# Edge weights from a second sort by run length, and the cell plan interleaved with the first convolution, in a graph network on one core

## The reference

```
h    = einsum('ni,rio->nro', x, weight)            # 8 transformed copies of each node
msg  = h[src, etype]
seg  = dst * R + etype
cnt  = segment_sum(ones, seg, N * R)               # edges per destination and type
norm = 1.0 / maximum(cnt[seg], 1.0)
agg  = segment_sum(msg * norm[:, None], dst, N)    # + x @ root + bias
# batch norm and relu after layers 0 and 1; x = layernorm(x + ...)
# then: h = x @ W_in + b_in; three times cur = segment_sum(cur[col] * w, row)
```

## Time and profile before

| | us |
|---|---|
| median of 3 runs | 5821.75 |
| lowest, highest | 5773.89, 5822.26 |
| profiled execution | 5815.68 |
| its span in the trace | 5813.9 |

### The profile page before, as it was taken

The page is one execution under the profiler, slowest core; times in us unless marked ns, Lnnn a source line. Parts: engine busy times, 40 slices in busy tenths (PEclk is TensorE's granted clock), DMA queues, the critical chain, the costliest instruction groups (busy, mean ns, idle before and its releaser), DMA issues.

```text
span 5813.9 us, 83767 instructions
## 1 busy us (share of the span) xinstructions
PE 4224.2 (73%) x16606; PEld 2206.6 (38%) x16607; DVE 3527.3 (61%) x10864; ACT 1456.7 (25%) x2714; POOL 2642.4 (45%) x2646
## 2 busy tenths in 40 slices
PE   7475576766766777677776786767677768989797
PEld 3122344444444333333333333333333333444343
DVE  8878644444445466666666556666666666364464
ACT  4465000000001333333333333333333340000000
POOL 0540466666665266666666436666666620000000
PEclk9678677777777998998899899998989889989898
DMA  6000111111111533333333353333334337969795
GB/s 215 8 11 6 30 45 45 45 45 45 45 45 41 200 120 118 118 119 119 118 119 118 123 196 116 119 119 119 119 117 120 117 109 248 301 225 301 234 300 170
DMA packets 416890, 716.88 MB, mean 123 GB/s; under 512 B 99201, under 2 KB 322742, under 8 KB 416330
## 3 DMA queue, kind: packets, MB, share of 16 engines
q1 hardware_dynamic: 332344, 545.52, 27.7%
q0 software_dynamic: 83984, 165.63, 11.4%
q10 hardware_dynamic: 130, 0.80, 0.0%
HBM read 431.69 MB, written 279.83 MB: 122 GB/s over the span
## 4 chain that ended last, share of the span: by engine, by line
PE 49%; issue 19%; DVE 14%; SPq 7%; another core or an unknown queue 5%; ACT 3%; DVEq 2%; DMA 1%; ACTq 0%
PE psum L961 15%; PE psum L1008 7%; PE psum L1009 7%; PE psum L948 6%; SPq L475 4%; PE psum L938 4%; SPq L476 3%; PE psum L909 3%; PE psum L842 2%; ACT bufE L655 2%; DVE area L1553 2%; PE psum L807 2%; DVE agg_and L1586 2%; DMA counts<-bufE 1%
## 5 line engine op out<-in xcount | busy, mean ns | idle before, releaser
L607 POOL DMA_INDIRECT area<-msg_table,visit_src x2490 | 2481.2, 996 | 1829.1 <-issue 581.4
L961 PE MATMUL psum<-area 128*128 128x256 f32 x4980 | 1713.8, 460 | 278.0 <-DVE agg_and L1586 247.0
L655 ACT CAST bufE<-psum 128x512 f16<-128x512 f32 x1507 | 883.3, 586 | 1761.3 <-PE psum L948 763.5
L961 PEld LDWEIGHTS psum<-area 128*128 128x128 f32 x4980 | 1046.5, 229 | 485.1 <-DVE agg_and L1586 279.4
L948 PE MATMUL psum<-bufE,carry 128*128 128x512 f16 x1506 | 643.6, 427 | 770.4 <-issue 461.7
L1586 DVE TENSOR_TENSOR agg_and<-agg_and,psum 128x256 f32 x1245 | 523.9, 421 | 770.6 <-PE psum L961 340.4
L1008 PE MATMUL psum<-area,edge_area 128*128 128x512 f16 (+1 forms) x1911 | 693.0, 370 | 81.2 <-DVE edge_area L1616 75.4
L948 PEld LDWEIGHTS psum<-bufE,carry 128*128 x1506 | 147.5, 98 | 1500.8 <-issue 1494.9
L1553 DVE SCALAR_TENSOR_TENSOR area<-iota,agg_and,psum 128x256 f32<-128x256 f32 x830 | 355.8, 478 | 558.6 <-remote 250.4
L1009 PE MATMUL psum<-area,edge_area 128*128 128x512 f16 (+1 forms) x1911 | 692.3, 370 | 0.0
L938 PE MATMUL psum<-bufE 128*128 128x512 f16 x1507 | 626.7, 416 | 0.7 <-issue 0.7
(11 more groups left out here) (318 smaller groups left out, 3077.1 us busy)
## 6 DMA issues: line engine op xcount, KB each, us to landing
area<-counts SPq DMA_DIRECT2D x252, 896.0 KB, 4.5
counts<-bufE SPq DMA_DIRECT2D x1507, 128.0 KB
msg_table<-area SPq DMA_DIRECT2D x147, 512.0 KB, 2.6
area<-msg_table,visit_src POOLq DMA_INDIRECT x2490
agg_and<-counts SPq DMA_DIRECT2D x162, 128.0 KB, 4.4
area<-counts SPq DMA_DIRECT2D x21, 224.0 KB, 3.4
bufE<-inv_sqrt SPq DMA_DIRECT2D x2, 1568.0 KB, 10.1
out<-cur SPq DMA_DIRECT2D x12, 256.0 KB
```

Source lines behind the costliest of these rows:

```text
L607: g.indirect_dma_start(out=msg[:, n % MV, :], out_offset=None, in_=msg_table, in_offset=bass.IndirectOffsetOnAxis(ap=visit_src[:, v:v + 1] ...
L655: a.copy(kept[:, m % KR, :], psum[:, 4 + m % 3, :]).then_inc(block_kept, 1)
L961: t.matmul(psum[:, banks[c % len(banks)], at:at + W2], msg[:, n % MV, :], visit_sel[:, n % SV, :], start=v % 2 == 0, stop=v % 2 == 1).then ...
```

## The change

1. `count_types`, its reciprocals, their way through DRAM, and in layer 0 the turning of types, their copies and the products with `inv_count` are gone.
2. In their place VectorE sorts the edges of each partition a second time, by destination, type and source (`group_edges`), and finds each run's length with one scan and ten shifted minima (`find_runs`). A run that crosses a partition's first or last destination is completed by counts of the eight types at both ends (`share_ends`), summed over partitions by four small products (`spread_ends`). The reciprocal is a third word of each edge.
3. Edges go to a new DRAM array `visit_rows` of three words, stored by ScalarE once the weights are known; GpSimd waits for that before the seven tile loads. `turn_tiles` turns three words instead of two, `keep_visits` copies `norm` out of PSUM.
4. `plan_cells` is cut into nine steps that run on VectorE after chunks 4, 14, ... 84 of layer 0, their TensorE products two chunks after each (`PLAN`, `plan_step`, `plan_product`).
5. Layer 0 uses four banks and adds three chunks late, as the other layers do, and selects with `norm`. The weights of layer 1 are made before `keep_visits`.
6. The ranking branch for unsorted edges is written anew, with two rounds; it is skipped with these edges. `load_tiles` no longer waits for the last addition of layer 0.

```diff
-MAIN = ((0, 1), (0, 1, 2, 3), (0, 1, 2, 3))
-SPREAD = (2, 3, 6)
+BANKS = (0, 1, 2, 3)
-LAG = (2, 3, 3)
+LAG = 3
+PLAN = tuple(range(4, 4 + 9 * 10, 10))
...
             pool.wait_ge(visits_planned, 1)
+            pool.wait_ge(rows_out, 16)
             for j in range(VB):
                 g.indirect_dma_start(out=runs[:, j, :, :].rearrange("p e w -> p (e w)"), out_offset=None,
-                                     in_=edge_rows.rearrange("(t e) w -> t (e w)", e=128),
+                                     in_=visit_rows.rearrange("(t e) w -> t (e w)", e=128),
...
             act.wait_ge(rows_ready, 1)
-            act.dma_start(edge_rows[0:E, :].rearrange("(p c) w -> p (c w)", p=EP), payload[:, :, :].rearrange("p c w -> p (c w)")).then_inc(rows_out, 16)
-            count_low()
-            keep_types()
+            act.dma_start(visit_rows[0:E, :].rearrange("(p c) w -> p (c w)", p=EP), edge_words[:, :, :].rearrange("p c w -> p (c w)")).then_inc(rows_out, 16)
...
+            def spread_ends():
+                pe.wait_ge(ends_ready, 1)
+                for j in range(2):
+                    last = t.matmul(psum[0:EP, 6, 128 * j:128 * j + EP], ones[0:EP, 0:EP], end_rows[:, j, :], start=True, stop=True)
+                last.then_inc(ends_spread, 1)
+                pe.wait_ge(shares_ready, 1)
+                for j in range(2):
+                    for h in range(2):
+                        last = t.matmul(psum[0:EP, 7, R * j:R * j + R], end_same[:, 2 * j + h, :], shares[:, 0, h, :], start=h == 0, stop=h == 1)
+                last.then_inc(shares_summed, 1)
...
                 for c in range(NQ):
+                    sums(c)
                     if k == 0:
-                        if c + 2 < NQ:
-                            turn_types(c + 2)
-                        if c + 1 < NQ:
-                            if (c + 1) % 2 == 0:
-                                pack = pack_of(c + 1)
-                            spread_weights(c + 1, pack)
-                    sums(c)
+                        plan_product(c)
...
+            def group_edges():
+                keys, spare = ungrouped.bitcast(I32), part(cur, 0, EC, dt=I32)
+                dve.wait_ge(x_turned, NXT)
+                link(v.tensor_scalar(keys[:, 0:EC], dst_i, GROUP_BITS + TYPE_BITS, KEY, ALU.logical_shift_left, ALU.bitwise_or))
+                link(v.tensor_scalar(spare, type_i, GROUP_BITS, None, ALU.logical_shift_left))
+                link(v.tensor_tensor(keys[:, 0:EC], keys[:, 0:EC], spare, ALU.bitwise_or))
+                link(v.tensor_tensor(keys[:, 0:EC], keys[:, 0:EC], src_i, ALU.bitwise_or))
+                link(v.memset(ungrouped[:, EC:SORT], NO_GROUP))
+                sort_keys(ungrouped, grouped)
+                keys = grouped.bitcast(I32)[:, 0:EC]
+                link(v.tensor_scalar(group_i, keys, GROUP_BITS, (1 << 16) - 1, ALU.logical_shift_right, ALU.bitwise_and))
+                link(v.tensor_copy(group, group_i))
...
+            def find_runs():
+                link(v.memset(same[:, 0:1], 0.0))
+                link(v.tensor_tensor(same[:, 1:EC], group[:, 1:EC], group[:, 0:EC - 1], ALU.is_equal))
+                link(v.tensor_tensor_scan(run_place, same, ones[0:EP, 0:1].to_broadcast([EP, EC]), 0.0, ALU.mult, ALU.add))
+                for buf in next_end:
+                    link(v.memset(buf[:, EC:1312], BIG))
+                frm, to = next_end
+                link(v.scalar_tensor_tensor(out=frm[:, 0:EC - 1], in0=same[:, 1:EC], scalar=BIG, in1=iota_visit[0:EP, 0:EC - 1], op0=ALU.mult, op1=ALU.add))
+                link(v.memset(frm[:, EC - 1:EC], float(EC - 1)))
+                for bit in range(LEVELS):
+                    link(v.tensor_tensor(to[:, 0:EC], frm[:, 0:EC], frm[:, 1 << bit:(1 << bit) + EC], ALU.min))
+                    frm, to = to, frm
+                link(v.tensor_tensor(run_place, run_place, iota_visit[0:EP, 0:EC], ALU.subtract))
+                link(v.tensor_tensor(run_place, run_place, frm[:, 0:EC], ALU.add))
+            def share_ends():
+                own, missing = shares[:, 0, :, :], shares[:, 1, :, :]
+                for j in range(2):
+                    for k in range(R):
+                        link(v.tensor_scalar(in_end[:, j, k, :], group, end_groups[:, j, k:k + 1], 0.0, ALU.is_equal, ALU.add, accum_out=own[:, j, k:k + 1]))
...
+            def find_norms():
...
+                for j in range(2):
+                    for k in range(R):
+                        link(v.scalar_tensor_tensor(out=run_place, in0=in_end[:, j, k, :], scalar=missing[:, j, k:k + 1], in1=run_place, op0=ALU.mult, op1=ALU.add))
+                v.reciprocal(edge_words[:, :, 2], run_place).then_inc(rows_ready, 1)
...
+            group_edges()
+            spread_ends()
+            find_runs()
+            share_ends()
+            decode_edges()
+            find_norms()
+            split_sources()
...
+            def plan_step(c):
+                if c == PLAN[0]:
+                    find_firsts()
+                elif c == PLAN[1]:
+                    find_cuts()
+                elif c == PLAN[2]:
+                    find_reach()
+                elif c == PLAN[3]:
+                    keep_dst_row()
...
+                elif c == PLAN[6]:
+                    find_tiles()
+                elif c == PLAN[7]:
+                    find_slots_of_blocks()
+                elif c == PLAN[8]:
+                    pack_carries()
...
-                        if k == 0:
-
-                            dve.wait_ge(weight_rows, q + 1)
-                            v.scalar_tensor_tensor(out=to, in0=iota[:, 0:W2], scalar=low, in1=psum[:, SPREAD[q % len(SPREAD)], at % 2 * W2:(at % 2 + 1) * W2],
-                                                   op0=ALU.is_equal, op1=ALU.mult, accum_out=norm[:, at:at + 1]).then_inc(visit_ready, 1)
-                        else:
-                            v.tensor_scalar(to, iota[:, 0:W2], low, norm[:, at:at + 1], ALU.is_equal, ALU.mult).then_inc(visit_ready, 1)
+                        v.tensor_scalar(to, iota[:, 0:W2], low, norm[:, at:at + 1], ALU.is_equal, ALU.mult).then_inc(visit_ready, 1)
...
+            make_weights(1)
             keep_visits()
```

495 lines of the change are left out of this document (222 added, 273 removed).

## The result

The changed kernel takes **5568.11 us** (median of 4 runs, 5565.44 to 5571.31), the kernel before 5803.24 (median of 4, 5773.89 to 5822.26) on the same chip: ratio **0.9596, 95% interval 0.9556 to 0.9637**. The prediction was 5424 with a range of 5355 to 5510. It is faster, as forecast, but by 235 us and not by 398 (the forecast started from a median of 5821.75).

What follows compares the result with a forecast made beforehand. No engine was near its limit; GpSimd lost time before the first gather and waiting for TensorE in layer 0. From 5815.7 us, 229.7 + 158.4 + 9.6 = 397.7 less gives 5418, plus 6 for the median: 5424, range 5355 to 5510.

Steps and rivals of the forecast that it cites:

- The preparation: Everything before layer 0's gathers: first gather at 400 us in place of 629.65, 229.7 us earlier.
- The scan: One scan of 800 elements on VectorE in finding runs: between 1.0 and 4.2 us, taken as 1.8.
- `rows_out`: GpSimd's added wait for stored edges before its tile loads: costs nothing, with 12 us to spare.
- The keys: GpSimd's key writes beside the sort: start 2.5 us earlier, slowed by 10 us (bounds nothing and 22), done at 373.5.
- Rival B: In the preparation, sort and key writes block each other: VectorE 82 us later, first gather 470, total 5494; chance 0.06.
- The last 5.7 us: End of the preparation: bases ready at 388 to 392, together with the tiles, then 9.2 us to the first gather at 400.
- Layer 0: First to last gather: GpSimd's pace of 1.284 us a gather stays, 1070 us in place of 1228.4, 158.4 us less.
- the bank rule: In layer 0, two banks keep TensorE from starting a chunk before the addition two chunks back; 247 us of waits, ended by four.
- The tail: From layer 0's last gather to its last addition: 6 us in place of 15.6, 9.6 less.
- A: Layer 0 keeps part of its pace through the chain of select, sum and addition: total 5454 to 5582; chance 0.17.
- D: The plan in layer 0 isn't hidden: 70 us of VectorE and 34 of TensorE on the path, total 5510; chance 0.05.
- C: Sorted rows make gather transfers slower in layers 0 to 2, so the kernel gets slower than before; chance 0.02.

Runs made afterwards that it cites:

- e7: Against the changed kernel, layer 0 sums into two banks and adds two groups behind, in place of four and three; layer 0 took 1196.6 us.
- e6: Against the changed kernel, TensorE in layer 0 waits for all four gathers and selections of a group before its first sum; layer 0 took 1196.7 us.
- f2: Against the changed kernel, VectorE makes 8 of the 256 columns of each selection in layer 0, for timing only; layer 0 took 1191.2 us.
- e2: Against the changed kernel, all plan steps and their products run ahead of the loop of layer 0; 5645.6 us, layer 0 1262.3 us.
- h1: The changed kernel itself, unaltered, run again on one chip with h2; 5568.41 us, ratio 0.9596 to the kernel before.
- h2: Against the changed kernel, 8 gather buffers in place of 16 and the degree count in layers 1 and 2 only; 5547.77 us, ratio 0.9565.
- f3: Against the changed kernel, TensorE in layer 0 sums only the last visit of each group of four, for timing only; layer 0 took 1188.9 us.

## Why the prediction was right and where it was wrong

**The preparation, right: 224.0 us earlier, 229.7 predicted.** Key writes by tile and GpSimd's timeline after, which answer to the earlier trace rows:

```profile
L547 POOL DMA_INDIRECT key_list<-edge_area x112: 1183/1191/1875, 188.3 to 377.7; - x112
```

```profile
379.17 0.98 POOL L603 DMA_INDIRECT bufE<-visit_rows,visit_tile  x1 [0.30 <-issue]
386.73 0.95 POOL L603 DMA_INDIRECT bufE<-visit_rows,visit_tile  x1 [0.30 <-issue]
405.69 0.95 POOL L577 DMA_INDIRECT area<-msg_table,visit_src  x1 [18.00 <-DVE agg_and L1547]
```

VectorE's timeline at the same place, and three groups of the preparation:

```profile
338.35 5.16 DVE L1335 RECIPROCAL bufD<-cur 125x800 f32<-125x800 f32 x1
386.15 1.66 DVE L1056 TENSOR_SCALAR area<-bases_sb,comp_sb 128x128 f32<-128x128 f32 x8 [40.58 <-DMA bases_sb<-in_L_gnn_bases]
387.84 7.51 DVE L1058 SCALAR_TENSOR_TENSOR area<-bases_sb,comp_sb,area 128x128 f32<-128x128 f32 x24
395.48 0.75 DVE L1533 MEMSET bufE<- 128x832 f32 x1
```

```profile
L1122 DVE TENSOR_TENSOR bufD<-bufD 125x512 f32<-125x512 f32 x55 | 38.5, 700 | 1.9
L1335 DVE RECIPROCAL bufD<-cur 125x800 f32<-125x800 f32 x1 | 5.2, 5155 | 0.0
L1290 DVE TENSOR_TENSOR_SCAN cur<-cur,ones 125x800 f32<-125x800 f32 x1 | 1.8, 1824 | 0.0
```

- The edges were ready at 343.51 us, where the reciprocal ends; predicted 346. The scan that the prediction bounded at 1.0 to 4.2 and took at 1.8 took 1.82, the reciprocal 5.16 (5.3 taken).
- `rows_out` cost nothing, as said: the first tile load follows the last key write by 0.30 us.
- The keys ended at 378.9, not 373.5. They started 4.6 us earlier (2.5 predicted), and 111 intervals took 189.4 us in place of 171.6: 18 us more, where 10 were taken, inside the bounds of 0 and 22. The sort steps themselves took 0.700 and 0.683 us, 0.693 and 0.685 before.
- Rival B (sort and keys block each other) did not come: not the step of VectorE is held up but the key write. Its mean was 1.43 us beside sort steps, 1.74 and 1.75 beside the 800-wide two-input steps L1334 and L1297, 1.19 beside the reciprocal. The Trainium skill, "SBUF — State Buffer", section "Who interferes with whom", names this pair. The trace agrees that the two contend, and not that whichever comes second is blocked for the whole instruction: sort steps beside a key write took 0.69 us, as without one, and the worst write, beside steps of 1.05 us, took 1.875 us against 1.19, 0.69 us more.
- The last 5.7 us: what ended last was the bases' path by way of SyncE, 395.4 in place of 388 to 392, because it hangs on the last key; from there to the first gather it was 10.3 us where 9.2 were taken.

**Layer 0, wrong: 32.0 us less, 158.4 predicted. This is the step that failed**: "TensorE no longer bounds it at either level, and four banks take away the wait of the earlier trace rows. GpSimd's pace is what stays ... 1.284 us". The measured 1196.4 us are 829 times the undisturbed interval of 1.252, 1038; 49 us by which gather instructions were longer than their median; and 110 of stops (predicted: 1065 with 17 of the second in it, and 5 for stops). The 49 are mostly the degree count: 1.62 us (mean of 45) for a gather beside its comparisons, 0.946 beside nothing; I had added 0.02 a gather from layer 1's mean. The 110 are the real error. In the kernel before GpSimd stood 1.1 to 2.2 us at 105 gathers, 86 of them exactly eighth ones, with two banks; I read the list of waits as the cause of these stops, and the bank rule as what would end them. They did end, and 48 irregular ones of 1.0 to 4.6 us took their place, 46 of them for the late signal of a sum that had long ended. e7 shows that the layer has the same length with the two banks kept. That signals can be late by the whole stock of buffers is in no term of the prediction.

**The tail, wrong sign:** 21.6 us, 15.0 before (the prediction counted 15.6, with the addition itself), 6 predicted. Last rows of layer 0:

```profile
1602.05 0.95 POOL L577 DMA_INDIRECT area<-msg_table,visit_src  x1 [0.31 <-issue]
1605.36 1.19 PE L905 MATMUL psum<-area 128*128 128x256 f32 x2 [0.74 <-DMA area<-msg_table,visit_src]
1611.08 0.42 DVE L1602 TENSOR_TENSOR agg_and<-agg_and,psum 128x256 f32 x1 [12.88 <-remote]
1622.38 0.42 DVE L1602 TENSOR_TENSOR agg_and<-agg_and,psum 128x256 f32 x1 [10.17 <-remote]
```

TensorE's last sum ended at 1606.55 by the records, "close behind the gathers" as predicted, but the addition could start only at 1622.38.

**The rivals.** A came true in its time (5454 to 5582) and in its place, and the "remote" waits named for it were the hint; I gave it 0.17. Its mechanism, a chain of select, sum and addition, is not it: e6, e7 and f2 change that chain and leave the pace. (The middle of its two ends is 5518, not 5510.) D (plan not hidden) is refuted by e2, C (slower transfers) by layers 1 and 2, which are unchanged, and by the packets, which end 2.2 to 2.3 us after a gather's start in both kernels.

**What stays open** is the cause of the 1.43 us. Shown: it is not TensorE's clock, load or number of sums, not banks, buffers, plan, degree count, VectorE's writes, the bytes moved or the time that a transfer takes; it stands in both layers without cell counts that were traced; GpSimd's stops end with late signals of sums, and how late these are follows the number of buffers while the layer's length doesn't. Not shown: why the signals are late, whether they and the pace have one cause, and what serves one gather in 1.43 us. Fewer rows a gather and the sums' code in a hardware loop were not tried.

## What to carry to other kernels

An engine's wait for another, in the list of waits, is not a price that goes when the wait is taken away: before counting it as gain, ask by a run or a second stage whether the pair could run faster at all. Here GpSimd in the stage with the other load (layer 1) already waited 224 us with four banks, and one kernel with two banks would have shown it. Deeper buffers that don't raise the pace only lengthened the tail of a stage: between h1 and h2, 8 gather buffers in place of 16 shortened the tails of layers 1 and 2 by 11 and 7 us. And the plan, moved into a loop in which the engines had 30% or more of their time idle, cost 3 to 8 us at most, against 66 ahead of it.

## What the runs showed of the hardware

- A matmul's recorded end, which the profile models, is not the time at which others see it. The lateness was 0.04 us (median) in layers with counts, and 10 us, at the extreme 43 with 32 buffers, in layers of sums alone, with TensorE busy 25 to 75% and at clocks from 0.51 to 0.73.
- The semaphore's own events show signals in bursts. In the changed kernel eleven sums ended between 704.0 and 716.6 us by the records; in that time the trace has one update, at 714.63, and then eight from 723.07 to 723.37, 0.04 us apart, and GpSimd's gather starts at 723.33. (The trace lacks some updates: it has 1773 of 2490.) Whether a sum or only its signal is late, this doesn't tell.
- In such stretches instructions come at multiples of 0.70 us. TensorE in the changed kernel, with data landed:

```profile
807.35 0.38 PE L905 MATMUL psum<-area 128*128 128x256 f32 x1 [1.71 <-issue]
808.75 0.59 PE L905 MATMUL psum<-area 128*128 128x256 f32 x1 [1.03 <-issue]
810.85 0.58 PE L905 MATMUL psum<-area 128*128 128x256 f32 x1 [1.52 <-issue]
812.95 0.59 PE L905 MATMUL psum<-area 128*128 128x256 f32 x1 [1.51 <-issue]
814.35 0.59 PE L905 MATMUL psum<-area 128*128 128x256 f32 x1 [0.81 <-issue]
```

  The starts are 1.40 or 2.10 us apart. In f3, where TensorE had little to do, it was VectorE: 215 of the 807 register instructions of one kind (ALU_OP) recorded there in layer 0 took 0.70 us in place of 0.045. In layers 1 and 2 SyncE has some 300 such register instructions each, in both kernels.
- A gather of GpSimd took 1.62 us (mean) beside a two-input comparison with a broadcast operand (L1589), 0.98 beside the one-input selection (L1572), 0.946 beside nothing.
